# Third stage of a vision-tower kernel: from rounds of two streams to a pipeline of single items

## The reference, cut to what matters

```
y   = w1 * expert_out[row1] + w2 * expert_out[row2]     # two gathered rows per token
h2  = h1 + LN3(x2 + y)
q, k, v = LN4'(h2) @ w_qkv + b_qkv                       # 8 heads of 16
att = softmax(q k^T / 4, keys within 32 tokens) @ v      # windowed attention
h3  = h2 + att @ w_att + b_att
xm  = LN5'(h3);  e = argmax(mean(xm) @ Wg + bg) of 16;  g = its softmax weight
out = h3 + g * (xm @ We[e] + be[e])                      # one expert for the whole image
```

## Time and profile before

| | before |
|---|---|
| median of 3 runs | 3326.36 us (3316.66 to 3330.95) |
| the profiled execution's own time | 3325.45 us |
| its span in the trace | 3323.6 us |
| PE busy (matmul) | 2877.9 us, 87% |
| PE weight loads | 2084.4 us, 63% |
| DVE busy | 1843.0 us, 55% |
| ACT busy | 1791.0 us, 54% |
| POOL busy | 1295.8 us, 39% |
| mean granted PE clock | 0.953 |

### The profile page before, as it was taken

The page is one execution under the profiler, slowest core; times in us unless marked ns, Lnnn a source line. Parts: engine busy times, 40 slices in busy tenths (PEclk is TensorE's granted clock), DMA queues, the critical chain, the costliest instruction groups (busy, mean ns, idle before and its releaser), DMA issues.

```text
span 3323.6 us, 79482 instructions
## 1 busy us (share of the span) xinstructions
PE 2877.9 (87%) x30591; PEld 2084.4 (63%) x30591; DVE 1843.0 (55%) x4178; ACT 1791.0 (54%) x3373; POOL 1295.8 (39%) x1252
## 2 busy tenths in 40 slices
PE   6999899999999949999999488888888888888887
PEld 4666666666666636666666366656566566665665
DVE  4888888888888851111111145545455455555555
ACT  4777677777767733333333155555455455555554
POOL 1465565565566550000000344444444444444430
PEclk9999999999999969999999799999999899999998
DMA  3222222222222014444555211111111111111110
GB/s 119 86 82 74 79 92 77 71 95 82 71 94 83 29 61 145 148 147 144 144 145 147 88 31 44 45 44 44 44 44 44 41 43 43 43 44 26 41 38 23
DMA packets 108625, 247.89 MB, mean 75 GB/s; under 512 B 21984, under 2 KB 39264, under 8 KB 104288
## 3 DMA queue, kind: packets, MB, share of 16 engines
q1 hardware_dynamic: 83808, 206.37, 19.2%
q0 software_dynamic: 24576, 37.80, 4.2%
HBM read 173.56 MB, written 70.52 MB: 73 GB/s over the span
## 4 chain that ended last, share of the span: by engine, by line
PE 60%; DVE 15%; issue 12%; ACT 7%; SPq 3%; POOL 1%; DMA 1%; DVEq 1%; another core or an unknown queue 0%; ACTq 0%; POOLq 0%
PE psum L502 9%; PE psum L1134 9%; PE psum L1145 9%; PE psum L1466 7%; PE psum L1562 4%; PE psum L1575 3%; PE psum L1551 3%; PE psum L1588 2%; DVE acc L794 2%; PE psum L537 2%; PE psum L229 2%; PE psum L1460 2%; PE psum L1528 2%; DVE unit L805 1%; DVE wsum L997 1%
## 5 line engine op out<-in xcount | busy, mean ns | idle before, releaser
L1393 POOL DMA_INDIRECT ycho<-expert_out,place x384 | 364.4, 949 | 1154.0 <-DVE place L1712 1071.4
L1032 POOL DMA_INDIRECT expert_in<-rows,slot_i x384 | 443.7, 1155 | 132.9 <-issue 110.4
L1175 ACT ACTIVATE hid<-psum,w_blk 128x512 f32<-128x512 f32 x320 | 219.8, 687 | 420.2 <-PE psum L1134 420.2
L1642 ACT ACTIVATE ex<-psum,smin 128x96 f32<-128x96 f32 x1152 | 295.3, 341 | 265.8 <-DVE smin L1755 198.6
L502 PE MATMUL psum<-xn,w_in 128*128 128x288 f32 x1024 | 299.5, 416 | 32.6 <-ACT rf L716 20.3
L1134 PE MATMUL psum<-x_t,w_blk 128*128 128x512 f32 x640 | 304.8, 609 | 1.6 <-DMA w_blk<-w_exp_in 1.6
L1145 PE MATMUL psum<-w_blk,hid 128*128 128x128 f32 x2560 | 299.2, 275 | 0.1
L1145 PEld LDWEIGHTS psum<-w_blk,hid 128*128 128x128 f32 x2560 | 292.3, 192 | 0.8 <-issue 0.5
L1762 DVE RECIPROCAL inv<-psum 128x64 f32<-128x64 f32 x288 | 159.8, 555 | 222.2 <-PE psum L1588 160.4
L1466 PE MATMUL psum<-keys,qdiag 32*32 32x96 f32 x9216 | 271.5, 251 | 9.4 <-issue 9.0
L1008 POOL TENSOR_TENSOR unit<-unit 128x576 f32<-128x576 f32 x64 | 133.1, 2080 | 375.1 <-ACT unit L669 258.4
(11 more groups left out here) (239 smaller groups left out, 5935.7 us busy)
## 6 DMA issues: line engine op xcount, KB each, us to landing
xin<-x_in SPq DMA_DIRECT2D x32, 1716.0 KB
w_blk<-w_exp_in SPq DMA_DIRECT2D x80, 578.0 KB, 4.3
rows_in<-expert_in SPq DMA_DIRECT2D x80, 256.0 KB, 3.4
expert_out<-rows_out SPq DMA_DIRECT2D x80, 256.0 KB, 4.3
h_dram<-h SPq DMA_DIRECT2D x32, 288.0 KB
x_dram<-x SPq DMA_DIRECT2D x32, 288.0 KB
h1c<-h_dram SPq DMA_DIRECT2D x32, 288.0 KB, 3.2
x2c<-x_dram SPq DMA_DIRECT2D x32, 288.0 KB, 3.5
```

The source lines that it names most:

```text
L1032: pool.indirect_dma_start(out=expert_in[:, :], out_offset=bass.IndirectOffsetOnAxis(ap=slot_i[z.s][:, n:n + 1], axis=0), in_=rows[z.s][:, ...
L1175: nc.scalar.activation(hid[s][:, c, :], HB[s][c % 2], ACT.Gelu_apprx_tanh, bias=w_blk[s][:, FF + FC * D + c:FF + FC * D + c + 1]).then_inc ...
L1393: pool.indirect_dma_start(out=ycho[s][:, k, :], out_offset=None, in_=expert_out[:, :], in_offset=bass.IndirectOffsetOnAxis(ap=place[s][:, ...
L1642: done = nc.scalar.activation(ex[s][u % 2][:, b, :], score_bank(u, s)[:, b * KW:(b + 1) * KW], ACT.Exp, bias=smin[s][u % 2][:, b:b + 1], s ...
```

## The change

All of `c_sync` to `c_vector` is written anew as a pipeline of single items. A step works on five items at once: v gathers its rows and forms the weighted sum, w has LN3 and LN4, x has queries, keys, values and attention up to the fifth unit's products, y has the last units of attention, projection, LN5 and the pick, and z the last layer. There are 36 steps; the hardware loop runs 12 times over two steps. One stream's PSUM (`A0`, `A1` = `P[0]`) serves all projections and layer norms, the other's four banks the attention of the one current item: two for scores, one for the transposes (`XB`), one for products and sums (`VB`). The SBUF tiles of a unit are rings of three. The code before the third stage changes only by dropping the shared layer-norm helpers.

Inside a unit, the sums are one matmul per partition group with an all-ones tile over all 128 columns, so that they come in the even/odd layout of the products; DVE picks products and sums together (128 columns instead of 64) and takes the reciprocal from SBUF. POOL spreads the 12 gathers between its nine `qdiag`s. The diff, cut to its core:

```diff
-                    for j in range(2):
-                        for t in range(NT):
-                            nc.tensor.matmul(sum_bank(s)[at], pair_ones[:, j, :],
-                                             ex_t[s][:, :, t * PH + j * QB:t * PH + (j + 1) * QB],
-                                             start=(j == 0), stop=(j == 1))
+                for t in range(NT):
+                    nc.tensor.matmul(sum_bank()[at], ones_k[:], ex_t[u % RING][:, :, at], start=True, stop=True)
...
-                    v.reciprocal(inv[s][:], sum_bank(s)).then_inc(head_step[s], 1)
-                    v.tensor_scalar(half[s][:], pv_bank(s)[:, :, 0, :], parity[:, 0:1], None, ALU.mult
+            def halves(x, u):
+                v.wait_ge(pv_done, x.upto(NU, u + 1))
+                v.tensor_scalar(half[:], both_heads(0), parity[:, 0:1], None, ALU.mult).then_inc(head_step, 1)
+            def heads(x, u):
...
+                v.scalar_tensor_tensor(out=one_head[:], in0=both_heads(1), scalar=parity[:, 1:2], in1=half[:],
+                                       op0=ALU.mult, op1=ALU.add).then_inc(head_step, 1)
+                v.wait_ge(head_step, x.upto(HEAD * NU, HEAD * u + 2))
+                v.reciprocal(inv[:], one_head[:, UB:, :]).then_inc(att_ready, 1)
+                v.wait_ge(att_ready, x.upto(2 * NU, 2 * u + 1))
+                v.tensor_tensor(att[x.s][:, u * UB * QB:(u + 1) * UB * QB].rearrange("p (b q) -> p b q", b=UB),
+                                one_head[:, 0:UB, :], inv[:], ALU.mult).then_inc(att_ready, 1)
...
+            with eng.Fori(C_LEAD // 2, ITERS - 1) as i:
+                for c in range(2):
+                    step(*[Item(i + (c - k) // 2, (c - k) % 2) for k in range(C_LAG + 1)])
...
+            def diagonal(x, u):
+                if u >= RING or x.old(1):
+                    pool.wait_ge(scores_done, x.upto(NU, u + 1 - RING))
...
+                for u in range(NU):
+                    if x:
+                        diagonal(x, u)
+                    if v and u:
+                        gather(v, range(3 * (u - 1) // 2, 3 * u // 2))
+                if v:
+                    weighted_sum(v)
...
+            def scores(x, u):
+                if u >= 2 or x.old(1):
+                    pe.wait_ge(ex_ready, x.upto(NU, u - 1))
+                pe.wait_ge(qdiag_ready, x.upto(NU, u + 1))
...
+            def turn(x, u):
+                if u or x.old(1):
+                    pe.wait_ge(ext_ready, x.upto(NU, u))
+                pe.wait_ge(ex_ready, x.upto(NU, u + 1))
...
+            def values(x, u):
...
+                if u or x.old(1):
+                    pe.wait_ge(head_step, x.upto(HEAD * NU, HEAD * u))
+                pe.wait_ge(ext_ready, x.upto(NU, u + 1))
```

More of the change, by code:

```diff
@@ L53 @@
 NU = IMGS * NQB // UB
-NI = 2 * IMGS
 E2 = 16
@@ L223, in hold @@
             eng.sem_inc(held["pool" if eng is nc.gpsimd else "sync"], 1)
[L227 to L247, removed]
         eps_col = sb("eps_col", [128, 2])
@@ L1385, in c_sync, with store, step @@
+            def store(x):
+                hold(sp, out_step, x.upto(IMGS + 1, IMGS + 1))
+                sp.dma_start(a["out"][:, a_range(x.n, x.s)], outs[x.s][:]).then_inc(out_stored[x.s], 16)
+            def step(v, w, x, y, z):
+                if v:
+                    load(v)
+                if y:
+                    experts(y)
+                if z:
+                    store(z)
+            c_steps(sp, step)
             for s in range(2):
@@ L1623, in c_tensor @@
-            c_steps(pe, trunk, attention, lambda i, more=True: None)
-            for s in range(2):
-                pe.wait_ge(tail_step[s], TAIL * ITERS)
-            nc.tensor.matmul(P[0][0][0:NI, 0, 0:E2], means[:], w_g[:], start=True, stop=True).then_inc(router_pe, 1)
-            last_layer(ITERS - 1)
+                                                qdiag[u % RING][at, b, :, :].rearrange("p j q -> p (j q)"),
+                                                keys[x.s][at, m, key_range(qb)], start=False, stop=(b == UB - 1))
@@ new lines, in router, with gates, last_layer @@
+            def router(x, bank):
+                pe.wait_ge(means_ready, x.upto(1, 1))
+                nc.tensor.matmul(bank[0:NI, 0, 0:E2], means[:], w_g[:], start=True, stop=True).then_inc(router_done, 1)
+            def gates(x, bank):
+                pe.wait_ge(pick_step, x.upto(PICK, PICK))
+                nc.tensor.matmul(bank[:, 0, 0:NI], C("ones")[0:NI, :], gdiag[:], start=True, stop=True
+                                 ).then_inc(gate_done, 1)
+            def last_layer(x, bank):
+                pe.wait_ge(wsel_landed[x.s], 16 * IMGS * (x.n + 1))
+                for m in range(IMGS):
+                    last = nc.tensor.matmul(bank[:, m // 2, (m % 2) * S:(m % 2 + 1) * S], wsel[x.s][:, m, 0:D],
+                                            four(xm[x.s][:])[:, m, :], start=True, stop=True)
+                last.then_inc(last_done, 1)
@@ L1695, in c_vector @@
+            c_steps(act, step)
         def c_vector(v):
```

959 lines of the change are left out of this document (475 added, 484 removed).

## The result

The changed kernel takes **3237.44 us** (median of 4 runs, 3231.58 to 3239.49) where the kernel before took 3327.01 beside it (4 runs, 3316.66 to 3330.95): ratio 0.9733, 95% interval 0.9707 to 0.9758. It is 2.7% faster. The forecast was 7.3%, 3083 us in a range of 3025 to 3195: the sign is right, the size is not, and the time lies above the range. The profiled execution took 3231.58 us, with a span of 3229.7.

The account below looks back on a forecast made before the run. PE was taken as the bound in attention, with about 24 us per round not PE work. A step of 31.8 + 0.7 + 1.3 + 1.3 = 35.1 us, times 32, plus fill, branch and drain, gave 3083 us, range 3025 to 3195.

Parts of the forecast that it names:

- the branch: Loop branch in stage three, once per two items: 12 x 1.9 = 22 us in the sum.
- rival C: POOL binds: spread gathers take 1.39 us each, steps up to 40.7 us, 3260 us in all; chance 0.08.
- the walk: One full step traced through its written orders with profiled durations, to find where PE waits.
- PE waits only some 0.7 us: Claim for PE in a full step, from its start up to scores(x,8) at 30.5 us.
- PE's work: PE's work for one item, attention units, projections, values, last layer and small pieces: 31.8 us.
- changes of form: Seven more switches of PE's tile form per step, each up to 0.18 us: 1.3 us per item.
- moe: PE's moe(v) near the end of a step waits 1.3 us for POOL's weighted sum.
- Sums and joint pick: In attention, softmax sums stay at 0.19 us; DVE's pick grows to near 1.9 us per unit.
- Not the bound by itself: DVE has 27 of 35 us of work per step, late only where a minimum follows a long wait.
- The clock: PE's clock in the 32 steps counted as full; if it falls, up to 2.6 us more per step.
- B: Rival: DVE's order binds, late links delay minima and later scores; step 38.7 us, 3200 us in all; chance 0.30.
- D: Rival: slower, only one attention unit under way at a time; step over 51 us, 3610 us; chance 0.05.

Follow-up runs that it names:

- c4: The changed kernel, unedited, run again in the fifth set of runs: 3164.27 us, against 3201.89 for the kernel before.
- e4: Changed kernel with the pick's logits in PSUM instead of SBUF, POOL's weighted sum left in place: 3211.93 us, against 3240.68 for the changed kernel.
- e7: Changed kernel with stage three written out as 36 steps, without loop or branch: 3208.43 us, against 3240.68 for the changed kernel.
- e9: Changed kernel with logits in PSUM, residual moved before minimum(5), and stage three without a loop: 3184.98 us, against 3270.83 for the changed kernel.
- sets 2 to 4: Three later sets of runs: unedited changed kernel 3244.62, 3240.68 and 3270.83 us; kernel before 3320.35, 3323.41 and 3379.66.
- e11: The kernel of e9 again, in the fifth set: 3067.54 us, against 3164.27 for the changed kernel.
- e8: Changed kernel with the old softmax sums and old separate picks put back: 3242.57 us, against 3240.68 for the changed kernel.
- e12: e11 with the old softmax sums and old picks put back: 3066.66 us, against 3067.54 for e11.
- b1: Kernel before plus only the all-ones softmax sums and joint pick, in the old rounds: 3262.79 us, against 3205.14 for the kernel before.
- set 5: Fifth set of runs: kernel before 3201.89 us, changed kernel unedited 3164.27 us.
- set 4: Fourth set of runs: kernel before 3379.66 us, changed kernel unedited 3270.83 us.

## Why the prediction was wrong in size

A full step should have taken 35.1 us, and 37.0 with the branch. In the first trace it took 39.3 and 42.6, on the mean 4.9 too much. In c4, without late releases, it took 37.6 and 41.0, 3.2 too much. So about 1.7 us of the 4.9 are the late releases, and 3.2 are steps of the forecast that fail without them as well.

- **POOL against DVE is the step that failed first.** The prediction had the shared interface before it, in rival C, and dropped it because "the weighted sum took 2747 to 2764 ns all 32 times, beside a busy or idle DVE". That row shows only that POOL's product loses nothing. It says nothing of DVE, nor of POOL's second instruction, the sum. The row to read was DVE's, in the trace of before:

```profile
L1775 DVE TENSOR_TENSOR att<-one_head,inv x288: 224/225/1304, 1947.4 to 3293.8; 128x64 f32<-128x64 f32 x144
```

In each of the 15 rounds one `att` begins inside POOL's product and takes 1.0 to 1.3 us, and one inside the sum takes 0.63. And the walk went through the pick without asking what stands beside it. It is worth 28.8 us by e4, 0.9 us per step, where releases are late. Where they are not (c4), PE waits for a sum that is 0.7 us longer.
- **The branch was priced at its old gap.** 12 x 1.9 was the gap alone. Removing it gave 32 us (e7), and more once `xq` was early: the gap is 3.15 us now, and the 1.8 us of slow work behind it were not in the sum. Together with the held pick (and the residual) this is 2.8 us per step in e9, of which 0.7 was counted.
- **"PE waits only some 0.7 us"** took `h3` at 1.29 and a minimum at 0.93. In the first trace and in sets 2 to 4 these two links are 1.0 to 1.6 us longer in every step: 1.8 us per step in the changed kernel, 2.8 by e9 against e11.
- **PE's work** was 31.8 plus 1.3 for changes of form. Projections were read off the weight-load queue as half of 1.77 us; start to start on the matmul queue a lone one is 1.07. Nine of them are 1.6 us more, so the work is 33.4. A projection takes the same 1.07 before transposes (2577.38 less 2576.31) as before the mask; whether a charge for the change of form is inside this 1.07 the rows can't tell, but nothing beside it is seen. The two errors nearly cancel, 1.6 against 1.3. That e11's full step lands on 35.1 is in part this luck: it is 33.4 of work, 0.8 of waiting for moe and 0.4 for exponentials, and 0.5 that I can't place, where the forecast had 31.8 of work, 1.3 for changes of form, 1.3 for moe and 0.7 of other waits.
- **Sums and joint pick:** "I take the 0.19 us of now" was right, since e8 and e12 show no difference in either direction. "Not the bound by itself" held for DVE, and b1 bears out that work of other items hides the longer pick.
- **moe** was forecast to wait 1.3 us for the sum. In the first trace it waits 0.4 in the step shown and 3.4 us in 25 steps, because PE is late itself; in c4 2.1 per step, and in e11 0.8.
- **The clock** was costed at full, with a bound of 2.6 us per step if a branch gap and the wait for moe should let it fall. The clock of the stage was 0.96 (0.94 in c4), and went to 1.00 in e9 and e11, whose gaps are gone. In c4 the fall behind the wait for moe is what happened: after it Q and the first values run at 1.2 GHz, 2.09 and 1.49 us to the next start (2560.73, 2562.82, 2564.31) for 1.07 and 0.88. That is 1.6 us per step, inside the bound, and the sum had it at nothing.
- Of the rivals, C's time of 3260 is nearest and B's 3200 next. C's picture did not occur: the gathers took 936 ns on the mean, not 1.39 us. B's picture (a late link delays a minimum) describes the late releases, but not the held pick or the branch. D did not occur.

The range missed because the shared port, the branch with its slow work and the late releases were each at nothing, or at less than half their size, in the sum, and B and C, whose times lay nearer, were left mostly outside. In set 5 the changed kernel's 3164 us lies inside the range, but beside a kernel before of 3202: a gain of 1.2%, further from the forecast 7.3% than the 2.7% of the result.

## What to carry to other kernels

When two engines may share a port, look for the loser in the rows of both engines: compare maximum and median of its short instructions, and ask which of them has two SBUF operands at the moment when the long POOL instruction will now run. If one of them is on the path, move an operand to PSUM; waiting with the POOL instruction or splitting it only moved the conflict here. And check the difference between intervals, not their mean alone: 39.3 and 42.6 by turns show the branch, 20.8 the fill. And after a new order, price the loop's branch by what PE does behind it, and test cures together: two that gave 27 and 32 us alone gave 86.

## What the runs showed of the hardware

- A DVE instruction of 64 elements with two inputs in SBUF took 2.70 us beside a POOL `tensor_tensor`, and 0.22 with one of its inputs in PSUM (e4), beside the same POOL instruction.
- POOL can be the one that loses: its sum of 96x768 took 2.53 us instead of 1.81 beside a DVE addition of 128x576 with both inputs in SBUF, which kept its 0.74 (c4).
- `half`, a `tensor_scalar` from PSUM, takes 184 ns with 64 columns (e8) and 345 with 128, while `one_head` goes from 281 to 347. A price per column read from one operation did not hold for the other.
- The same kernel took 3185 us in set 4 (e9) and 3068 in set 5 (e11), at a granted clock of 1.00 in stage three both times. 88 of the 117 us (31 x 2.83) are in the steps of stage three, where two receivers of PE's signals per step are released 1.1 to 1.6 us earlier in the faster one. Another 25 us come before the first `prec` (1908.4 against 1883.7), in stages one and two, which no edit touches.
